# A conditional attention block whose two ends are reordered

## Chip, core and metric

One core of a Trainium2 chip. The time is that of the device in microseconds (us). Three runs of the kernel before gave 372.36, 374.06 and 375.03 us (median 374.06). The profile is one further execution.

## What is computed

For each of 16 batches x (256 tokens, 256 features), with one conditioning vector w per batch:

```
gamma, beta = w @ Wg.T + bg, w @ Wb.T + bb          # one row of 256 per batch
sln(h)  = gamma * ((h - mean) / sqrt(var + 1e-5) * ln_g + ln_b) + beta
q, k, v = sln(x) @ Wqkv.T + bqkv                    # 16 heads of 16 features
att     = softmax(q @ k.T) / 16 @ v
h1      = att @ Wp.T + bp + x
out     = sln(h1) + h1
```

All inputs and the output are float32. The kernel keeps that precision with matmuls in fp32r, by splitting each operand into a high part (the fp32r rounding) and a low part (what is left): three matmuls stand for one product. For the scores the four combinations of parts are stacked in the 128 rows of one contraction, and two more rows of it subtract the row maximum.

## The kernel before

Every engine has its own instruction list, written out by hand; semaphores join them. TensorE (PE) multiplies and transposes, ScalarE (ACT) takes exponentials and copies PSUM to SBUF, VectorE (DVE) takes maxima, norms and low parts, GpSimd (POOL) does small work on SBUF, SyncE (SP) issues most transfers. Each list runs in its order; an instruction that waits holds all behind it on its engine.

**Steps.** After a set-up, `steps(step, last=B + 2)` runs step b = -1 to 17 on every engine, each with 16 slots h, one per head. In step b PE computes the scores of batch b, head h, into `st0` or `st1` in turn (L838), and the same products for batch b+1 into `sa0` or `sa1` (`scores_max`, L825), of which DVE takes the row maxima (L573). ACT's exponential (L512) empties the score bank. `weigh` (L849) multiplies four heads' exponentials with V, three slots later, into `pv0` (heads 0 to 7) or `pv1`. The other work of neighbouring batches has fixed slots (L46 to L54): projections of Q and K of batch b+2 (L799) and of V of batch b+1 (L808), the transposes of the maxima (L889), `out_by_token` (L873), the transposes of `att`, the output projection of batch b-1 (L817), and gamma and beta of batch b-2 as rows of `gb` (L965). `between` (L713) is the same table for DVE: `residual` stages 0 to 5 are the sum h1, its statistics, mean and variance, epsilon, and the two halves of the second norm; `norm1` is the first norm; `low_qk`, `low_att` and `low_max` are low parts; `normalise` divides by the softmax sum.

**Stacks.** `qst` and `kst` hold the stacked parts of Q and K. `stack(a, g, t)` on SP (L267) sends the high parts of batch a, half g of the heads, t = 0 for Q and 1 for K, in two transfers of 128 KB, waits for the low parts and sends them in two more. For batch 0, K goes by ACT's queue (`stack_k0`, L530). POOL issues the two small transfers of the maxima rows (`maxima`, L315; `m_h` and `m_l`), which the scores of that half wait for (L842). The transfers of batch 1's first half go out in step -1, of its second half in step 0.

**Set-up.** PE keeps busy with matmuls on zeros (`warm_up`, 9 and 5 of them: `WARM`), waits for all of `vectors`, `cond`, `wg` and `wb` (`cond_in`, L1010), transposes the vectors, multiplies gamma and beta into one bank, transposes the normed x of batch 0 (`turn_x(0)`), then projects Q and K of batch 0 (`project_first`) once `hTl_ready` says that the low part of h is there. Then follow the transposes of gamma and beta to rows, `turn_x(1)`, the bias product `Wp.T @ bv + bp` (`rows_bias`, L905), and Q of batch 1. K of batch 1 comes in slots 0 to 3 of step -1. ACT rounds the weights and zeroes `qst` in four `clear_q` (L516), the last behind `high_q(1)`.

**End.** In step 15 there is no batch 16 to take maxima of: PE has scores, weighs, transposes and the projection of batch 14. Steps 16 and 17 hold the end of batch 15: last weigh, `evict_out`, transposes, `normalise`, transposes, `aT_h`, `low_att`, projection, `residual`. The rows `gb` of batches 14 and 15 are multiplied and copied there too, each ahead of the `h1b` sum on POOL (L377) that it is needed for.

Of the kernel before, what the change touches and what calls it, by code (L numbers as in the profile page):

```python
# [32 lines left out]
P = 128  # L33
# [15 lines left out]
WARM = (9, 5)  # L49
# [4 lines left out]
S_OT1, S_OT0 = 5, 13  # L54


def cond_block(nc, x, condT, vectors, WgT, WbT, WqkvT, WpT, bp, out):
    with ExitStack() as ctx:
# [27 lines left out]
        gb_part = sb("gb_part", [P, KT, B])  # L86
        gfull = sb("gfull", [P, KT, B])
# [32 lines left out]
        gb = sb("gb", [P, 2 * D])  # L120
        h1 = sb("h1", [P, TT, D])
# [11 lines left out]
        cond_in = sem("cond_in")  # L133
# [6 lines left out]
        max_in = [[sem(f"max_in{g}{p}") for p in range(2)] for g in range(2)]  # L140
        qpad_ready = sem("qpad_ready")
# [19 lines left out]
        gbpart_ready = sem("gbpart_ready")  # L161
        gfull_ready = sem("gfull_ready")
# [46 lines left out]
        h1_ready = sem("h1_ready")  # L209
        ln2_step = sem("ln2_step")  # L210
# [27 lines left out]

        def xbuf(a):

            return xa[:, a % NX]

        def steps(body, first=-1, last=B + 1):

            for b in range(first, last):
                body(b)
# [7 lines left out]
        def _(sp):  # L254
            wqkv_t = WqkvT.rearrange("(k p) n -> p k n", p=P)
            sp.dma_start(xbuf(0), x_t[0]).then_inc(x_in[0], 16)
            sp.dma_start(vrows[:], vectors).then_inc(cond_in, 16)
            sp.dma_start(cond[:], condT.rearrange("(k p) n -> p k n", p=P)).then_inc(cond_in, 16)
# [8 lines left out]
            def stack(a, g, t):  # L267

                if not has(a):
                    return  # L270
# [5 lines left out]
                s, p = stack_in[g][par(a)], par(a)  # L276
                dst, hi, lo = (qst, kst)[t], qk_h[:, p, t, g, :], qk_l[:, p, t, g, :]
                wait(sp, (qh_ready, kh_ready)[t], 1 * a + 1)
                for n in (0, 2) if t == 0 else (0, 1):
                    sp.dma_start(raw(dst[PART_ROW[n]:P:P // HD, p, g * HH:(g + 1) * HH, :]), raw(hi)).then_inc(s, 16)  # L280
                wait(sp, (ql_ready, kl_ready)[t], 1 * a + 1)
                for n in (1, 3) if t == 0 else (2, 3):
                    sp.dma_start(raw(dst[PART_ROW[n]:P:P // HD, p, g * HH:(g + 1) * HH, :]), raw(lo)).then_inc(s, 16)

            def step(b):
                if not first(b + 1):
                    stack(b + 1, 1, 0)
                    stack(b + 1, 1, 1)
# [4 lines left out]
                stack(b + 2, 0, 0)  # L293
                stack(b + 2, 0, 1)
# [11 lines left out]
            for p in range(2):  # L306
                sp.wait_ge(y_out[p], 16 * (B // 2))
# [760 lines left out]
```

## Time and profile before

| | us |
|---|---|
| median of three runs | 374.06 |
| the profiled execution's own time | 374.8 |
| its span, first to last instruction | 373.0 |
| PE busy | 351.7 (94%) |
| DVE busy | 305.7 (82%) |
| ACT busy | 248.7 (67%) |
| POOL busy | 162.8 (44%) |

Busy shares are means over stages that differ. The page's slices show that both ends are thinner than the middle (tenths of 40 equal slices, and PE's granted clock in tenths of full speed):

```profile
PE   8788999999999999999999999999999999999960
DVE  2779877789888888899898888888898978886563
ACT  6434677767776776777676767767776767677710
PEclk9969999999999999999999999999999999999975
```

"Granted clock" is 1.00 where PE may run at 2.4 GHz and 0.50 at 1.2 GHz. An idle time in brackets is that of the engine just before the group, with what ended it.

### The profile page before, as it was taken

Reading aid. Unit: us, or ns where it says so; the run is one execution under the profiler, and the core shown is the slowest. Engines: PE = TensorE matmul, PEld = TensorE weight load, DVE = VectorE, ACT = ScalarE, POOL = GpSimd, SP = SyncE. Lnnn points to the kernel's source line nnn. Section 1 sums busy time; section 2 is a strip of 40 time slices with the busy share of each in tenths; the row PEclk is TensorE's granted clock in tenths of the full one; section 3 lists DMA queues with packets and bytes.
Section 4 is the critical chain, followed back from the end, with each engine's and each line's share of the span. In section 5 each row is a group of like instructions: output and inputs, shape, how many; then the busy total and the mean of one; then the engine's idle time right before and its main releaser. Section 6 shows DMA issues by size and latency. Waiting matters only on the chain.

```text
span 373.0 us, 8969 instructions
## 1 busy us (share of the span) xinstructions
PE 351.7 (94%) x3161; PEld 291.4 (78%) x3161; DVE 305.7 (82%) x729; ACT 248.7 (67%) x487; POOL 162.8 (44%) x203
## 2 busy tenths in 40 slices
PE   8788999999999999999999999999999999999960
PEld 5566778888888888888888889888888888787640
DVE  2779877789888888899898888888898978886563
ACT  6434677767776776777676767767776767677710
POOL 6616443327262725435262627254352634062242
PEclk9969999999999999999999999999999999999975
DMA  7095445444354444555544544444554443410000
GB/s 265 28 219 153 108 117 144 117 137 123 111 142 123 127 121 126 143 145 143 143 105 126 143 123 127 115 134 140 144 142 118 108 136 102 133 45 30 31 28 28
DMA packets 45258, 44.69 MB, mean 120 GB/s; under 512 B 6015, under 2 KB 40846, under 8 KB 45214
## 3 DMA queue, kind: packets, MB, share of 16 engines
q1 hardware_dynamic: 41470, 42.02, 40.7%
q10 hardware_dynamic: 1696, 1.57, 1.7%
q0 software_dynamic: 2048, 0.53, 0.9%
q8 instruction: 25, 0.41, 0.5%
q14 instruction: 19, 0.16, 0.1%
HBM read 5.79 MB, written 4.19 MB: 27 GB/s over the span
## 4 chain that ended last, share of the span: by engine, by line
PE 88%; DVE 5%; issue 2%; ACT 2%; DMA 1%; POOL 0%; POOLq 0%; DVEq 0%; ACTq 0%
PE m L791 24%; PE pv L791 20%; PE st L791 19%; PE sa L791 17%; PE pv L880 4%; PE pv L988 2%; PE m L920 1%; DVE mx L573 1%; PE m L894 1%; DMA qst<-m_l 1%; ACT p L512 1%; DVE qk_l L608 1%; PE pv L894 0%; DVE y L689 0%; DVE xn L635 0%
## 5 line engine op out<-in xcount | busy, mean ns | idle before, releaser
L573 DVE TENSOR_REDUCE mx<-sa 128x2 f32<-128x512 f32 x256 | 171.9, 678 | 40.6 <-PE sa L791 39.8
L512 ACT ACTIVATE p<-st 128x512 f32<-128x512 f32 x256 | 150.8, 599 | 58.3 <-PE st L791 57.7
L791 PE MATMUL st<-qst,kst 128*128 128x256 f32 x512 | 111.9, 301 | 1.2 <-DMA qst<-m_l 0.6
L791 PE MATMUL sa<-kst,qst 126*128 126x256 f32 x512 | 104.8, 286 | 2.2 <-DVE mx L573 1.9
L791 PEld LDWEIGHTS st<-qst,kst 128*128 128x128 f32 x512 | 77.8, 189 | 29.0 <-ACT p L512 16.4
L791 PEld LDWEIGHTS sa<-kst,qst 126*128 126x128 f32 x512 | 79.4, 191 | 4.1 <-DVE mx L573 4.0
L323 POOL DMA_DIRECT2D qst<-m_h x32 | 18.1, 566 | 118.3 <-DVE m_l L582 118.3
L791 PE MATMUL pv<-p,v_st 128*32 128x256 f32 x1024 | 68.5, 385 | 0.3 <-ACT p L512 0.3
L791 PEld LDWEIGHTS pv<-p,v_st 128*32 128x32 f32 x1024 | 26.7, 109 | 20.0 <-ACT p L512 0.5
L791 PE MATMUL m<-hT_h,wqkv_h 128*128 128x256 f32 x128 | 38.6, 310 | 0.3 <-DVE hT_l L652 0.3
L791 PE MATMUL m<-hT_l,wqkv_h 128*128 128x256 f32 x128 | 35.8, 288 | 0.0
L791 PE MATMUL m<-hT_h,wqkv_l 128*128 128x256 f32 x128 | 35.6, 287 | 0.0
L332 POOL TENSOR_SCALAR xn<-xa,mv,rstd 128x256 f32<-128x256 f32 x28 | 34.0, 1216 | 0.4
L350 POOL TENSOR_TENSOR hT_l<-hT,hT_h 128x512 fp32r<-128x512 f32 x14 | 17.9, 1278 | 35.8 <-ACT hT_h L426 35.8
L364 POOL TENSOR_TENSOR rstd<-vare,minus_half 128x4 f32<-128x4 f32 (+1 forms) x19 | 17.3, 908 | 33.5 <-DVE vare L630 19.4
L462 ACT ACTIVATE oT<-pv 128x512 f32<-128x512 f32 x32 | 19.2, 599 | 15.9 <-PE pv L791 15.9
L608 DVE SCALAR_TENSOR_TENSOR qk_l<-m,vecs,qk_h 128x256 fp32r<-128x256 f32 x64 | 27.6, 473 | 2.1 <-ACT qk_h L442 2.1
L791 PEld LDWEIGHTS m<-hT_h,wqkv_h 128*128 128x128 f32 x128 | 24.9, 199 | 1.9 <-issue 1.9
L791 PEld LDWEIGHTS m<-hT_h,wqkv_l 128*128 128x128 f32 x128 | 24.5, 195 | 0.6
L791 PEld LDWEIGHTS m<-hT_l,wqkv_h 128*128 128x128 f32 x128 | 24.6, 197 | 0.0
L689 DVE SCALAR_TENSOR_TENSOR y<-h,mv,gb 128x256 f32<-128x256 f32 x32 | 24.4, 801 | 0.0
L791 PE MATMUL m<-wp_h,aT_h 128*128 128x256 f32 x64 | 20.0, 312 | 2.1 <-DVE aT_l L658 2.1
(104 smaller groups left out, 574.1 us busy)
## 6 DMA issues: line engine op xcount, KB each, us to landing
qst<-qk_h SPq DMA_DIRECT2D x64, 128.0 KB, 2.4
qst<-qk_l SPq DMA_DIRECT2D x64, 128.0 KB, 2.5
kst<-qk_h SPq DMA_DIRECT2D x60, 128.0 KB, 2.5
kst<-qk_l SPq DMA_DIRECT2D x60, 128.0 KB, 2.8
xa<-x_dram SPq DMA_DIRECT2D x16, 256.0 KB, 3.1
out_dram<-y SPq DMA_DIRECT2D x16, 256.0 KB, 2.1
wqkv<-WqkvT_dram SPq DMA_DIRECT2D x1, 512.0 KB, 5.3
kst<-qk_h ACTq DMA_DIRECT2D x4, 128.0 KB, 4.3
```

The source lines that it names most:

```text
L323: pool.dma_start(raw(qst[MAX_ROW + r:MAX_ROW + 1 + r, p, g * HH:(g + 1) * HH, :]) .rearrange("a h (t n) -> a (h t) n", t=TT), raw(m[:, g, ...
L332: o = pool.tensor_scalar(xn[:, t, :], xbuf(a)[:, t, :], mv[:, t, 0:1], rstd[:, 0, t:t + 1], ALU.subtract, ALU.mult)
L350: pool.tensor_tensor(hT_l[:, par(a)], hT[:], hT_h[:, par(a)], ALU.subtract).then_inc(hTl_ready, 1)
L364: pool.tensor_tensor(rstd[:, which], vare[:, which], minus_half[:, which], ALU.pow).then_inc(rstd_ready, 1)
L462: nc.scalar.activation(oT[:, g, :], pv_ps[g][:], ACT.Copy).then_inc(oT_ready, 1)
L512: nc.scalar.activation(p32[:, h % PR, :], st_ps[h % 2][:], ACT.Exp).then_inc(exp_done, 1)
L573: dve.tensor_reduce(mx[:, par(a), h // HH, (h % HH) * TT:(h % HH + 1) * TT], sa_ps[h % 2][:].rearrange("p (t n) -> p t n", t=TT), AX.X, AL ...
L608: o = dve.scalar_tensor_tensor(out=qk_l[:, par(a), t, g, :], in0=ps[:, g * N:(g + 1) * N], scalar=vecs[:, 4 + t, g:g + 1], in1=qk_h[:, par ...
L689: o = dve.scalar_tensor_tensor(out=y[:, par(a), t, :], in0=h1[:, t, :], scalar=mv2[:, t, 0:1], in1=gb[:, 0:D], op0=ALU.subtract, op1=ALU.mult)
L791: return nc.tensor.matmul(o, l, r, start=start, stop=stop)
L880: o = nc.tensor.transpose(pv_ps[g][:, t * N + c * P:t * N + (c + 1) * P], oT[:, g, c * N + t * P:c * N + (t + 1) * P], ident[:])
L988: o = nc.tensor.transpose(pv_ps[1][:, k * N + t * P:k * N + (t + 1) * P], att[:, t, k * P:(k + 1) * P], ident[:])
```

## The change

At the head:

- Loads: `cond` is issued ahead of `vectors`; three semaphores (`vrows_in`, `wg_in`, `wb_in`) take the place of `cond_in`. gamma and beta get a bank each. Their bias terms are worked out beforehand (`gb_add`), so bfull is one sum.
- PE's warm-ups are 8 and 4. `project_first` starts when the high part of h is there, and takes the low part after that. `rows_bias` moves ahead of `turn_x(1)`, and `bias_cols` on DVE far ahead. Q of batch 1: two quarters before step -1 and two in slots 0 and 1; K in slots 2 to 5; V of batch 0 in slots 9 and 10 (`V_FIRST`) instead of 7 to 9. The transpose of the first maxima goes to `pv1`.
- ACT: the fourth `clear_q` and the high part of the V weights move ahead of `high_q(0)`, the copy of the bias ahead of `high_q(1)`, `high_k(1)` from slot 4 to 6. ACT, not POOL, issues the first maxima rows.
- DVE: `low_qk` of K of batch 0 passes ahead of the norm of batch 1; both `low_qk` of batch 1 move from slots 1 and 5 to 8 and 9, behind the eight maxima of the first half.
- SP: `send` is one quarter of a stack; all high parts of batch 1 go out ahead of its low parts, and its second half in step -1. POOL fills `kst` of batch 1 in one piece ahead of `rstd_x(1)`.

At the end:

- Steps run to 15, and an ending is written out for each engine. In step 15 DVE makes the four copies from PSUM (oT twice, gb, aT_h) that ACT made, and the projection of batch 14 stands in slots 10 to 12 (`P_LAST`).
- The rows of gamma and beta for batches 14 and 15 are made in step 14 (`gb_t`, `S_GT`).
- Batch 15's second group of heads is handled by halves: its two weighs go to two banks; eviction, transposes, normalise, transposes and `aT_h` work on four heads or on one 128-row part; the projection adds the first part early (`project_half(0)`), then four warm-ups, then the second. h1, h1b, the last y and the output go by halves of the tokens.

```diff
-WARM = (9, 5)
+WARM = (8, 4)
+V_FIRST = (9, 9, 10, 10)
+WARM_END = 4
+P_LAST = (10, 11, 11, 12)
+S_GT = (4, 11)
...
-            stack(0, 0, 0)
-            stack(0, 1, 0)
-            steps(step, last=B + 2)
+            for g in range(2):
+                for low in range(2):
+                    send(0, g, 0, low)
+            for t in range(2):
+                for g in range(2):
+                    send(1, g, t, 0)
+            for t in range(2):
+                send(1, 0, t, 1)
+            steps(step)
+            wait(sp, y_ready, B - 1)
+            sp.dma_start(out_t[B - 2], y[:, par(B - 2)]).then_inc(y_out[par(B - 2)], 16)
+            for t in range(TT):
+                sp.wait_ge(yt_ready, t + 1)
+                sp.dma_start(out_t[B - 1][:, t, :], y[:, par(B - 1), t, :]).then_inc(y_out[par(B - 1)], 16)
...
+                    if h == S_MT0 + 1 and first(b + 1):
+                        for r, m, ready in ((0, m_h, mh_ready), (1, m_l, ml_ready)):
+                            act.wait_ge(ready, 1)
+                            act.dma_start(raw(qst[MAX_ROW + r:MAX_ROW + 1 + r, 0, 0:HH, :])
+                                          .rearrange("a h (t n) -> a (h t) n", t=TT),
+                                          raw(m[:, 0, :])).then_inc(max_first, 16)
...
             high_h_direct(0)
             clear_q(1, 0)
+            clear_q(1, 1)
+            act.wait_ge(wv_in, 16)
+            nc.scalar.activation(wqkv_h[:, :, 2 * D:3 * D], wqkv[:, :, 2 * D:3 * D], ACT.Copy).then_inc(wvh_ready, 1)
             act.wait_ge(vecs_ready, 1)
             high_q(0)
...
-                    between[(1, 0)] = [lambda: low_qk(1, 0, m0, qh_ready, ql_ready)]
-                    between[(5, 0)] = [lambda: low_qk(1, 1, m1, kh_ready, kl_ready)]
-                    between[(9, 0)] = [lambda: low_max(0, 0)]
+                    between[(8, 0)] = [lambda: low_qk(1, 0, m0, qh_ready, ql_ready), lambda: low_max(0, 0)]
+                    between[(9, 0)] = [lambda: low_qk(1, 1, m1, kh_ready, kl_ready)]
+                if last(b):
+                    between[(3, 1)] = [lambda: evict_out_last(b - 1, 1)]
+                    between[(4, 1)] = [lambda: evict_rows_last(b - 2)]
+                    between[(9, 1)] = [lambda: high_att_last(b - 1), lambda: low_att(b - 1)]
+                    between[(11, 0)] = [lambda: evict_out_last(b, 0)]
+                    between[(12, 1)] = [lambda: residual(b - 1, 0)]
+                    between[(15, 0)] = [lambda: residual(b - 1, 1)]
+                    between[(15, 1)] = [lambda: residual(b - 1, 2), lambda: residual(b - 1, 3)]
...
+            low_att_half(0)
+            residual(B - 2, 4)
+            normalise_half(0)
+            normalise_half(1)
+            residual(B - 2, 5)
+            low_att_half(1)
+            wait(dve, xdb_ready, B)
+            wait(dve, h1b_ready, B - 1)
+            for t in range(TT):
+                wait(dve, projt_done, t + 1)
+                dve.tensor_tensor(h1[:, t, :], st_ps[t][:, 0:D], xbuf(B - 1)[:, t, :], ALU.add).then_inc(h1t_ready, 1)
...
+            weigh(B - 1, 2)
+            pe.wait_ge(att_ready, 2 * B - 1)
+            for t in range(TT):
+                o = nc.tensor.transpose(sa_ps[1][:, t * P:(t + 1) * P], att[:, t, 0:P], ident[:])
+            o.then_inc(aT0_done, 1)
+            weigh(B - 1, 3)
...
+            project_half(0)
+            pe.wait_ge(attt_ready, 2)
+            for t in range(TT):
+                o = nc.tensor.transpose(pv_ps[1][:, t * P:(t + 1) * P], att[:, t, P:2 * P], ident[:])
+            o.then_inc(aT1_done, 1)
+            pe.wait_ge(h1_ready, B - 1)
+            for _ in range(WARM_END):
+                mm(m1[:], zeros[:, 0:P], zeros[:], True, True)
+            project_half(1)
```

## Rows read from the trace of the kernel before

**Rows 1.** Stretches (us); busy time and count of each engine, granted clock, DMA.
```profile
39.10:319.00 279.90, 279.70 (x2657) 238.38 (x2658) 244.18 (x582) 203.22 (x411) 126.63 (x148) 1.00 0.47 128
...
340.00:354.20 14.20, 13.47 (x124) 9.10 (x122) 7.29 (x19) 11.08 (x22) 4.80 (x6) 1.00 0.06 21
```
**Rows 2.** In order of time, set-up: start, length, engine, line, operation.
```profile
1.46 4.02 PE L791 MATMUL sa<-zeros 128*128 128x512 bf16 x9 [1.46 <-DVE zeros L746]
...
5.41 0.18 PEld L1012 LDWEIGHTS pv<-ident,vrows 14*128 14x128 f32 x1 [0.84 <-DMA cond<-condT_dram]
...
9.06 1.09 PE L920 MATMUL st<-ident,xn 128*128 128x128 f32 x4
...
10.07 0.36 DVE L763 SCALAR_TENSOR_TENSOR bfull<-pv,vecs,gb_part 128x16 f32<-128x16 f32 x2
...
12.62 1.20 PE L791 MATMUL m<-hT_h,wqkv_h 128*128 128x256 f32 x4 [0.34 <-DVE hT_l L652]
...
16.00 0.84 ACT L442 ACTIVATE qk_h<-m,vecs 128x256 fp32r<-128x256 f32 x2 [2.59 <-PE m L791]
```
**Rows 3.** Stretches again, where PE idles or runs at the lower clock.
```profile
16.80:19.30 2.50, 0.02 (x1) 0.00 (x0) 2.42 (x5) 0.77 (x3) 1.99 (x4) 1.00 0.32 78
...
20.50:22.30 1.80, 1.73 (x5) 0.99 (x5) 0.71 (x2) 0.93 (x2) 0.00 (x0) 0.61 1.13 223
...
25.50:27.50 2.00, 2.00 (x11) 1.94 (x10) 1.10 (x3) 1.10 (x3) 0.57 (x1) 0.50 1.10 223
...
360.30:362.00 1.70, 1.69 (x8) 1.69 (x9) 0.75 (x2) 0.00 (x0) 0.00 (x0) 0.50 0.05 17
```
**Rows 4.** In order of time, 17 to 29 us.
```profile
17.67 1.58 DVE L635 TENSOR_SCALAR xn<-xa,mv,rstd 128x256 f32<-128x256 f32 x2
...
20.07 1.20 ACTq L535 DMA_DIRECT2D kst<-qk_l  x2
...
27.12 1.91 ACT L516 ACTIVATE qst<-ones 128x2048 fp32r<-128x2048 f32 x1
```
**Rows 5.** Instructions on tile `kst`, 16 to 28 us: its transfers.
```profile
DMA to landing us min/median/max: 3.2/4.7/5.5
```
**Rows 6.** In order of time, step -1 and the first scores.
```profile
26.96 0.69 DVE L573 TENSOR_REDUCE mx<-sa 128x2 f32<-128x512 f32 x1 [0.87 <-PE sa L791]
...
30.86 0.88 DVE L608 SCALAR_TENSOR_TENSOR qk_l<-m,vecs,qk_h 128x256 fp32r<-128x256 f32 x2
...
31.65 1.97 DVE L573 TENSOR_REDUCE mx<-sa 128x2 f32<-128x512 f32 x3
...
33.87 0.69 DVE L573 TENSOR_REDUCE mx<-sa 128x2 f32<-128x512 f32 x1 [0.25 <-PE sa L791]
...
34.70 4.55 DVE L573 TENSOR_REDUCE mx<-sa 128x2 f32<-128x512 f32 x7
...
38.20 1.27 POOL L350 TENSOR_TENSOR hT_l<-hT,hT_h 128x512 fp32r<-128x512 f32 x1 [1.90 <-ACT hT_h L426]
...
39.10 0.50 PE L791 MATMUL st<-qst,kst 128*128 128x256 f32 x2 [0.58 <-DMA qst<-m_l]
```
**Rows 7.** In order of time, step 15 and the end.
```profile
342.88 0.39 PE L791 MATMUL pv<-gb_hl,pick_b 128*128 128x512 f32 x1
...
353.63 0.60 ACT L512 ACTIVATE p<-st 128x512 f32<-128x512 f32 x1 [0.84 <-PE st L791]
...
354.28 1.07 PE L791 MATMUL pv<-p,v_st 128*32 128x256 f32 x16 [0.34 <-ACT p L512]
...
357.39 2.26 DVE L689 SCALAR_TENSOR_TENSOR y<-h,mv,gb 128x256 f32<-128x256 f32 x2
...
364.01 0.75 DVE L674 BATCH_NORM_STATS2 stats<-h 128x6 f32<-128x256 f32 x2
...
367.57 0.88 DVE L697 SCALAR_TENSOR_TENSOR y<-y,rstd,h1b 128x256 f32<-128x256 f32 x2 [1.53 <-POOL h1b L377]
```
**Rows 8.** The page's part 6, DMA issues: KB each, median us to landing.
```profile
out_dram<-y SPq DMA_DIRECT2D x16, 256.0 KB, 2.1
```

More of the change, by code:

```diff
@@ L237, in par, with max_sent, last, steps @@
             return a % 2
+        def max_sent(a, g):
+            return 32 * (half(a) + (1 if g or par(a) else 0)) if a >= 0 else 0
+        def last(a):
+            return a == B - 1
         def xbuf(a):
             return xa[:, a % NX]
-        def steps(body, first=-1, last=B + 1):
+        def steps(body, first=-1, last=B):
             for b in range(first, last):
@@ L275, in stack @@
                     sp.wait_ge(kpad_ready, a + 1)
[L276 to L283, printed above, removed]
+                wait(sp, ((qh_ready, ql_ready), (kh_ready, kl_ready))[t][low], 1 * a + 1)
+                src = (qk_h, qk_l)[low][:, p, t, g, :]
+                for n in (low, low + 2) if t == 0 else (2 * low, 2 * low + 1):
+                    sp.dma_start(raw((qst, kst)[t][PART_ROW[n]:P:P // HD, p, g * HH:(g + 1) * HH, :]),
+                                 raw(src)).then_inc(s, 16)
+            def stack(a, g):
+                if not has(a):
+                    return
+                for t in range(2):
+                    for low in range(2):
+                        send(a, g, t, low)
             def step(b):
-                if not first(b + 1):
-                    stack(b + 1, 1, 0)
-                    stack(b + 1, 1, 1)
+                if has(b - 1) or has(b) and not first(b):
+                    stack(b + 1, 1)
                 if has(b + 4) and has(b):
@@ L465, in step @@
                 for h in range(H):
-                    if h == S_O1:
+                    if h == S_O1 and not last(b):
                         evict_out(b - 1, 1)
-                    if h == S_O0:
+                    if h == S_O0 and not last(b):
                         evict_out(b, 0)
-                    if h == S_GB + 1 and has(b - 2):
+                    if h - 1 in S_GT and last(b + 1):
+                        i = S_GT.index(h - 1)
+                        wait(act, gbt_done, i + 1)
+                        nc.scalar.activation(gb_t[:, i, :], m0[:], ACT.Copy).then_inc(gbt_ready, 1)
+                    if h == S_GB + 1 and has(b - 2) and not last(b):
                         wait(act, gb_done, 1 * (b - 2) + 1)
@@ L841, in scores @@
                 if h % HH == 0:
-                    wait(pe, max_in[h // HH][p], 32 * (half(b) + 1))
+                    if first(b) and h == 0:
+                        pe.wait_ge(max_first, 32)
+                    else:
+                        wait(pe, max_in[h // HH][p], max_sent(b, h // HH))
                 wait(pe, exp_done, 16 * b + h - 1)
@@ L851, in weigh @@
                 p, g, c = par(b), q // 2, q % 2 * N
+                bank = pv_ps[g]
+                if last(b) and q == 3:
+                    bank, c = m0, 0
                 wait(pe, exp_done, 16 * b + 4 * q + 4)
@@ L858, in weigh @@
                     wait(pe, att_ready, 2 * b + g - 1)
+                if last(b) and q == 3:
+                    pe.wait_ge(gbt_ready, 2)
                 if q == 0:
@@ L947, in step @@
                     a, j = (b, h - LAG) if h >= LAG else (b - 1, h - LAG + H)
-                    if has(a) and j % 4 == 3:
+                    if has(a) and j % 4 == 3 and not (last(a) and j // 4 == 2):
                         weigh(a, j // 4)
```

251 lines of the change are left out of this document (190 added, 61 removed).

## The prediction

> **What bounds the kernel now.** I read busy time by stretches first, then the instructions in order of time at both ends. From 39.1 to 319 us TensorE (PE) is busy 279.7 of 279.9 us at full granted clock, and in the last full batch (step 15, 340.0 to 354.2) 13.5 of 14.2 us [rows 1]. The change leaves the steps between alone, so I forecast nothing there. What can move is the 39.1 us ahead of the first score matmul, step 15, and what follows it: the last weigh starts at 354.28, the last y ends at 367.57 + 0.88 = 368.45 [rows 7], the span at 373.0.
>
> **Head, first part.** PE's transpose of `vrows` sat 0.84 us behind the `cond` transfer [rows 2]. Now it waits for `vrows` alone, and one 0.43 us warm-up is gone (nine took 4.02 us): PE is 0.4 us ahead. gamma and beta keep their eight matmuls each, so `turn_x(0)` ends at 9.75 instead of 9.06 + 1.09 = 10.15 [rows 2]. The bfull chain (old end 10.43) loses its common wait: gamma work runs beside the beta matmuls, and the four small operations added on DVE (2 on gb_add, 2 for bias_cols, some 0.8 us) run before gamma arrives at 7.2. So `hT` starts at 9.85 rather than 10.48. The first projection now asks for hT_h (about 11.05: two ACT halves after 9.85), where hT_l released it at 12.62 [rows 2]; four warm-ups of 0.43 from 9.6 end near 11.3. Up to Q's eviction at 16.00 PE needed 3.4 us [rows 2]; started 1.3 us earlier, with more of them at the low clock, I let its matmuls end 1.2 us earlier, Q at 14.8 and all 24 at 15.2.
>
> **ACT gives half of that back.** Ahead of `high_q(0)` it now has a second `clear_q` of 1.91 us (old place 27.12 [rows 4]) and the V weights' high part (128 x 512, 0.6 like an exp of that size [rows 7]). 11.05 + 1.9 + 1.9 + 0.6 = 15.45 against 16.00 [rows 2]: 0.55 us ahead. Then `low_qk` of K passes ahead of the 1.58 us of xn [rows 4]: ACT's queue, which stands on kl_ready, issues kst<-qk_l at 18.7 instead of 20.07 [rows 4], and gets to hT_h(1) 1.3 us sooner. Hence hT_l(1) is ready at 21.95 instead of 23.3. PE starts Q of batch 1 at 22.05. Of its twelve matmuls (0.21 each at granted 0.50: eight in 1.69 us [rows 3]) only six stand ahead of the first maxima. SP issues the same transfers in another order: batch 0 first, then all high parts of batch 1. Nothing that batch 0 needs is behind a later wait. The last K part for heads 0 to 7 is issued by 19.95; landings took 3.2 to 5.5, median 4.7 [rows 5], so 23.1 to 25.4. I take 23.5, since the two engines issue the same bytes 0.5 us sooner: PE begins the maxima at 23.5, DVE at 24.0 where it began at 26.96 [rows 6].
>
> **Bias in PE's gap.** PE sat idle 2.5 us from 16.8; at 20.5 to 22.3 the clock had fallen to 0.61 on average, at 25.5 to 27.5 it was 0.50, that is 1.2 GHz [rows 3]. The six bias matmuls now fill about 15.9 to 17.3, which hides them; without that gap they would cost those 1.4 us. Idle remains: 17.3 to 19.0 for xn, 19.6 to 22.05 for hT_l, 4.1 us in two pieces against one of 2.5 and a short one: I take it that the clock still falls. The Trainium skill, "TensorE: Matmul & The Clock Gate", section "What's actually happening", says that activity releases the throttle and that the moment of the change is not tied to the kernel's start and varies from run to run; by it the gap's outcome can differ between runs of one program. That is the first rival.
>
> **First step (maxima of batch 0).** At 1.2 GHz a head with 2 sa and 3 projection matmuls costs PE 1.07 us, DVE's maximum takes 0.655 (1.97/3 [rows 6]). Three or four heads go at PE's pace, the rest at DVE's: the eighth maximum ends near 30.5. Before it was 31.65 + 1.97 = 33.6 with two `low_qk` (0.87, 0.88 [rows 6]) in front; a shift of -3.1. Those two now stand behind it: +1.75 back, and the 0.25 us that DVE waited ahead of the ninth [rows 6], with V matmuls in PE's slot 7, goes away. V moves to slots 9 and 10, under DVE's extra 0.88. The maxima rows go out by ACT's queue directly; m_l was written ahead of the seven maxima that start at 34.70, and its transfer released the first scores at 39.10 after 0.58 us of idle [rows 6]; now m_l is there at 31.2 against a need at 37.4, so that transfer leaves the path even at 5.5 us. Next late are DVE's last seven maxima (4.55 us) and hT_l(2) on POOL, 38.20 + 1.27 = 39.47 [rows 6], which moves with the ninth maximum. Both shift by -3.1 + 1.75 - 0.25 = -1.6. K's low part of batch 1 is ready at 33.1, issued by 34.5 and needed at 37.5; a landing of 3.2 from 33.9 fits, one of 5.5 would cost 2. **Head: -1.6 us**, bounds +0.1 and -2.8.
>
> **Step 14.** Two more 512-column matmuls for gb_t with their loads: the like one took 0.39 from start to end [rows 7]; overlapped with its neighbours I charge a little over half, 0.22, and PE is the bound: +0.45, from 0 to 1. ACT's two copies lie in its third of idle time; SP and POOL get one small copy each way.
>
> **Step 15.** ACT had 16 exps of 0.60 [rows 7], and between them copies of the same 128 x 512 for oT, gb, aT_h and oT. Four copies to DVE (about 0.69 each, what a maximum over the same bank takes [rows 6]) take 2.4 us from ACT. But score banks are two, and PE's weighs (1.07) already hold the exps up; following the two-bank rule head by head, the last exp starts at 352.85 instead of 353.63 [rows 7]. The projection of batch 14 moves up into slots 10 to 12 and eats what the copies give. weigh(15,2) moves behind the loop but before weigh(15,3), so that one ends at about 355.0 instead of 354.28 + 1.07 = 355.35: only 0.4 gained here.
>
> **Tail, by halves.** Before, from 355.4: oT, transposes, rec, att, transposes, aT_h, then DVE was held by y of batch 14 (2.26 us, started 357.39, twice its free 0.88 [rows 7]), aT_l, 12 matmuls at granted 0.50 (from 360.31 on, [rows 3]), h1, statistics, y, POOL's rstd and h1b (DVE idle 1.53 on it), last y. After, in the same clock: second half of oT 355.0 to 355.4, its transposes to 355.8. DVE: low_att_half(0) 354.4 to 354.8, y of 14 from 354.8. POOL adds h1b(14) at 354.6 to 355.8, so I charge the slowed pair, 1.9, not 0.88: to 356.7. Two normalise halves, an estimate of 0.55 each: 357.8. Transposes, aT_h half: 358.6. Second y of 14 (0.87) runs meanwhile; low_att_half(1) to 359.05. The first half of the projection and four warm-ups cover PE's wait, so PE idles under 1.5 us at a time and I keep the clock at full: six matmuls 0.7 (half of 6 x 0.21, and a little), with h1 (2 x 0.4) started after three: 360.35. Statistics, aggregate, vare: 1.2 us, as from 364.01 on [rows 7], 361.6; y 0.88 to 362.5. POOL's h1b halves run during the statistics, rstd (0.88) beside y. Last y 362.5 to 363.4. Old 368.45: -5.05, of which 0.4 is step 15, 1.4 the earlier projection, 1.9 its half length and full clock, 1.4 h1b off the path. Output follows: 256 KB took 2.1 from issue [rows 8]; two of 128 KB, the second no earlier than the last y: 0 to -1, I take -0.3. **Step 15 and tail: -5.35**, bounds -3.7 and -6.3 (y of 14 free of POOL: another -0.95).
>
> **Sum.** -1.6 + 0.45 - 5.35 = -6.5 us. The profiled run took 374.8 (span 373.0 and 1.8 around it), 0.74 above the median of three; 374.8 - 6.5 = 368.3 on its terms, 367.6 on the median's.
>
> **Rivals.**
> Clock stays up in the head (0.17): the bias fill leaves shorter gaps; for it speaks the 1.00 that still stood at the end of 2.5 us of idle, against it the 0.50 after [rows 3]. Then DVE paces all 16 maxima from 23.5, eighth at 29.3: -2.8 in the head, 366.4.
> Tail only (0.13): batch 1's low parts land late, or K's landing eats the start; the head's -1.6 is nil: 369.2.
> Clock drops in the tail (0.13): the four warm-ups become 1.7 us, outlasting DVE's 359.05 by 0.8, and six matmuls cost 0.6 more: -5.35 becomes -3.95, 369.0; with DVE's in-order queue also late by a us, 370.2.
> No effect (0.06): the ends are as long as before because something I take for hidden is not, 373 to 375.
> Slower (0.04), one mechanism: with 12 warm-ups instead of 14 before 11.3 us and less dense work, PE's clock does not rise and steps 0 on run at 0.50. In a PE-bound step each us spent at half clock loses half a us; against a gain of 6.5, 13 us of it turn the sign. The row of 25.5 to 27.5 shows that busy PE can stand at 0.50 [rows 3]; full clock over all of 39.1 to 319 speaks against. At 21 us of it, a step: 378.
> The rest (0.47) is the sum as it stands.
>
> **Numbers.** 1% is 3.7 us, about what can be told from no change. Faster by more, under 370.3: the sum 0.47, clock up 0.17, tail only 0.12, most of the clock drop 0.07: 0.83. Within 1%: 0.12; slower: 0.05. Range 364.4 to 371.2: the gain bound of both ends (-2.8 - 6.3) sits just outside at the low side, the double miss in the tail inside at the high side.
>
> **What would show it.** PE's first projection near 11.3 and ending near 15.2; qk_h at 15.4; first maximum at 24, the eighth ended at 30.5, scores at 37.5 with hT_l(2), not a transfer, as PE's releaser; granted clock between 20 and 27. The last exp should start 12.8 us after step 15's first scores, and the last y end 10.5 us behind it (14.8 before). In the tail: y of 14 at 1.9, PE's clock at the second half projection, POOL no longer named ahead of the last y. A head shift of zero, or step 15 no shorter, would make the forecast wrong.

## The result and the profile after

The changed kernel took 368.32 us (median of four runs, 368.09 to 369.82) against 374.54 for the kernel before: the ratio is 0.985, with an interval of 0.980 to 0.990. That is 1.5% faster, 6.2 us. The forecast was 367.6, 364.4 to 371.2. The profiled execution took 368.27, with a span of 366.4: 6.6 us under the profiled one before.

The page's first part after (busy us, share, instructions). Of the 6.6 us of span, 4.6 are PE's busy time (351.7 before; nearly the same number of instructions, fewer of them at the lower clock) and 2.0 its idle time; DVE is busy for 4.5 us more than before.

```profile
PE 347.1 (95%) x3162; PEld 288.1 (79%) x3163; DVE 310.2 (85%) x738; ACT 247.0 (67%) x485; POOL 161.9 (44%) x202
```

The head after, in order of time, with the instructions that answer to [rows 2] and [rows 6]:

```profile
5.81 0.23 PE L1201 MATMUL pv<-ident,vrows 14*128 14x14 f32 x1 [0.85 <-DMA vrows<-vectors_dram]
5.97 1.06 PE L960 MATMUL pv<-cond,wg 128*128 128x16 f32 x8
...
8.33 1.91 PE L960 MATMUL sa<-zeros 128*128 128x512 bf16 x4
...
10.06 1.85 PE L960 MATMUL m<-hT_h,wqkv_h 128*128 128x256 f32 x8
...
13.98 0.83 ACT L517 ACTIVATE qk_h<-m,vecs 128x256 fp32r<-128x256 f32 x2
...
22.03 0.64 PE L960 MATMUL sa<-kst,qst 126*128 126x256 f32 x2
...
24.84 4.10 DVE L668 TENSOR_REDUCE mx<-sa 128x2 f32<-128x512 f32 x6 [0.38 <-PE sa L960]
...
35.02 1.28 POOL L401 TENSOR_TENSOR hT_l<-hT,hT_h 128x512 fp32r<-128x512 f32 x1 [4.68 <-ACT hT_h L498]
35.18 0.40 PE L960 MATMUL st<-qst,kst 128*128 128x256 f32 x2
...
36.35 0.39 PE L960 MATMUL m<-hT_h,wqkv_h 128*128 128x256 f32 x1 [0.26 <-POOL hT_l L401]
```

The eighth maximum ends at 28.94 (before 33.6), the first scores wait for no transfer, and the first projection of step 0 starts at 36.35 with `hT_l` as its releaser, which is the releaser that was forecast; before, it started at 39.69.

How the lead then runs on is best read at one instruction that comes twice in each step: PE's transpose of the maxima. Of its 32 times I give the lead over the kernel before (worked out as the difference of the two traces): 3.23 us in step 0, 3.27 at 125.5 us, 3.04 from 136.4 us on, 2.96 when step 14 begins, 2.58 at its end (340.7 before, 338.12 after). So 0.23 is lost in one piece in step 4 and 0.38 in step 14. The start of the last weigh is 1.81 ahead (354.28 before, 352.47 after): another 0.77 is lost in step 15. It has two parts. From the first scores of step 15 to the last exp it is 351.21 - 337.44 = 13.77 us, where it was 353.63 - 340.02 = 13.61: 0.16 lost. From the last exp to the start of the last weigh it is 1.26 instead of 0.65, another 0.61, since the weigh of the third group and two transposes now stand between them. The last y is 6.37 ahead, the span 6.6. The end therefore gained 4.56 behind the start of the last weigh, and step 15, which was to gain, lost.

Step 15 and the end after, by engines, in order of time; the part of it that answers to [rows 7]:

```profile
341.77 1.29 POOL L432 TENSOR_TENSOR h1b<-h,gb 128x512 f32<-128x512 f32 x1
...
342.76 3.44 DVE L789 SCALAR_TENSOR_TENSOR y<-h,mv,gb 128x256 f32<-128x256 f32 x2
343.01 1.27 POOL L392 TENSOR_TENSOR xa<-xa,bias_b 128x512 f32<-128x512 f32 x1
...
344.25 1.27 POOL L472 TENSOR_TENSOR xa<-xa,bias_b 128x512 f32<-128x512 f32 x1
...
346.13 0.68 DVE L818 CAST aT_h<-pv 128x512 fp32r<-128x512 f32 x1
...
347.58 0.39 PE L960 MATMUL m<-wp_h,aT_h 128*128 128x256 f32 x1 [1.14 <-DVE aT_l L753]
...
348.48 0.60 ACT L597 ACTIVATE p<-st 128x512 f32<-128x512 f32 x1 [2.40 <-PE st L960]
...
352.47 1.07 PE L960 MATMUL m<-p,v_st 128*32 128x256 f32 x16
...
353.34 1.69 DVE L789 SCALAR_TENSOR_TENSOR y<-h,mv,gb_t 128x256 f32<-128x256 f32 x2
...
355.96 0.44 PE L1248 MATMUL pv<-ident,att 128*128 128x128 f32 x2 [0.76 <-DVE att L928]
...
357.33 0.38 PE L960 MATMUL st<-wp_h,aT_h 128*128 128x256 f32 x1
...
361.20 0.88 DVE L954 SCALAR_TENSOR_TENSOR y<-y,rstd,h1b 128x256 f32<-128x256 f32 x2 [0.30 <-POOL rstd L488]
```

The reader should follow one line of cause: POOL makes three whole additions one behind the other from 341.77 to 345.52; DVE's pair of y, 0.88 when alone, takes 3.44; DVE's copy of aT_h, next in its queue, comes at 346.13, so PE stands 1.14 us for aT_l, and with it the next scores: ACT idles 2.40 us ahead of an exp. The run "POOL late" below tests this.

### The profile page after: what moved, and what is told of

Same layout as the page of the kernel before. It is cut to its first block, busy times and chain, and to the rows that moved or that the text cites. A ratio compares the mean times of both kernels' runs of the same rounds, so it can differ in the third digit from the quotient of the medians.

```text
span 366.4 us, 9039 instructions
## 1 busy us (share of the span) xinstructions
PE 347.1 (95%) x3162; PEld 288.1 (79%) x3163; DVE 310.2 (85%) x738; ACT 247.0 (67%) x485; POOL 161.9 (44%) x202
## 3 DMA queue, kind: packets, MB, share of 16 engines
q10 hardware_dynamic: 1760, 1.59, 1.6%
## 4 chain that ended last, share of the span: by engine, by line
PE 85%; DVE 5%; ACT 3%; DMA 2%; issue 1%; ACTq 1%; POOL 1%; SPq 0%; POOLq 0%; DVEq 0%
PE m L960 24%; PE st L960 19%; PE pv L960 18%; PE sa L960 16%; PE pv L1057 4%; PE pv L1169 2%; PE m L1097 2%; DMA wqkv<-WqkvT_dram 2%; DVE mx L668 1%; DVE y L789 1%; PE m L1071 1%; ACT qst L601 1%; ACTq L620 1%; ACT p L597 1%; ACT hT_h L611 0%
## 5 line engine op out<-in xcount | busy, mean ns | idle before, releaser
L960 PE MATMUL pv<-p,v_st 128*32 128x256 f32 x1008 | 67.5, 385 | 0.0
L537 ACT ACTIVATE oT<-pv 128x512 f32<-128x512 f32 x29 | 17.4, 599 | 14.0 <-PE pv L960 14.0
L415 POOL TENSOR_TENSOR rstd<-vare,minus_half 128x4 f32<-128x4 f32 (+1 forms) x17 | 15.7, 923 | 19.2 <-DVE vare L725 19.1
L789 DVE SCALAR_TENSOR_TENSOR y<-h,mv,gb 128x256 f32<-128x256 f32 x28 | 23.2, 866 | 0.0
L960 PE MATMUL m<-wqkv_h,hT_h 128*128 128x256 f32 x64 | 19.3, 301 | 0.2 <-DVE qk_l L703 0.2
```

The lines of the kernel that those rows point to most:

```text
L415: pool.tensor_tensor(rstd[:, which], vare[:, which], minus_half[:, which], ALU.pow).then_inc(rstd_ready, 1)
L537: nc.scalar.activation(oT[:, g, :], pv_ps[g][:], ACT.Copy).then_inc(oT_ready, 1)
L789: o = dve.scalar_tensor_tensor(out=y[:, par(a), t, :], in0=h1[:, t, :], scalar=mv2[:, t, 0:1], in1=gam[:, 0:D], op0=ALU.subtract, op1=ALU. ...
L960: return nc.tensor.matmul(o, l, r, start=start, stop=stop)
```

## The experiments

Each run's time is a median, of four runs (ten for head only, five for best); "before" is the kernel before, measured together with it. Runs of one edited kernel differ by up to 2.4 us (368.00 to 370.36 for "loads together"), so medians a few tenths apart tell nothing. Where tenths count I use two distances inside each trace, since the time also holds the head's luck (below). The first is from the first maxima matmul to the first projection of step 0 ("step -1"); the second from the transpose of batch 15's second maxima, a little into step 15, to the start of the last y ("end"). In the changed kernel they are 36.35 - 22.03 = 14.32 and 361.20 - 338.12 = 23.08 us. The six traces with the changed kernel's very ending have 23.08 to 23.10, so the second repeats to a few hundredths; the first varies from 14.06 to 14.62 in the twelve with its order of step -1.

| run | time | before | step -1 | end | first maxima |
|---|---|---|---|---|---|
| before | 374.54 | | 13.53 | 26.87 | 26.16 |
| changed | 368.32 | 374.54 | 14.32 | 23.08 | 22.03 |
| head only | 372.92 | 374.06 | 14.39 | 26.9 | 22.93 |
| POOL late | 368.51 | 374.06 | 14.33 | 21.9 | 23.64 |
| ACT copies | 368.41 | 374.06 | 14.06 | 22.3 | 23.88 |
| no end warm-ups | 370.03 | 374.06 | 14.46 | 23.1 | 23.69 |
| both | 367.53 | 374.57 | 14.14 | 22.3 | 22.08 |
| halves first | 366.28 | 374.57 | 14.62 | 21.0 | 22.17 |
| low parts early | 370.95 | 374.57 | 15.71 | 23.1 | 23.80 |
| wait for hT_l | 369.59 | 374.57 | 14.23 | 23.1 | 23.01 |
| bias late | 369.83 | 373.18 | 14.39 | 23.1 | 23.79 |
| vectors first | 368.44 | 373.18 | 14.54 | 23.1 | 22.27 |
| loads together | 369.27 | 373.18 | 14.54 | 23.1 | 23.66 |
| best | 365.91 | 373.18 | 14.42 | 21.0 | 21.99 |

**Head alone.**

```diff
-            return a == B - 1          # last(a)
+            return False
-        def steps(body, first=-1, last=B):
+        def steps(body, first=-1, last=B + 2):
```
and the written-out endings of all engines, `gb_t` and its `pick_t` are taken out.

> The head of the change with the end of the kernel before (steps to 17, ACT's evictions, whole batch 15, POOL as before). If the two ends simply add, step 0 starts as early as in the changed kernel (first scores near 35.2, 3.3 us ahead at the first projection of step 0), the end costs what it did, and the time is 3.2 us under the kernel before: 371.3. If what the head gained beyond my 1.6 us is the luck of the clock in one run, the lead at step 0 is 1.6 to 2 us here: 372.7. If the head's lead is given back in the steps between, the second-half maxima transposes of later batches lose it again: 374.

Measured: 372.92, ratio 0.9958 (0.9936 to 0.9981) over ten runs, so 1.1 to 1.6 us, near my second theory's time (372.7), though the trace leads by 2.27 us in step 0, more than the 1.6 to 2 of that theory. It keeps the lead to the end, 2.39 at the last transpose: nothing is given back when the changed end is absent. In the traces the two ends add. The changed kernel's span is 370.43 - 366.44 = 3.99 us shorter: 0.96 is a faster head in that execution, 3.80 the end (26.88 against 23.08), and 0.77 goes off for steps 4 and 14. So the end with what it costs is worth 3.0 us. The difference of the medians, 372.92 - 368.32 = 4.6, is larger, since the two sets of runs also differ in the head's luck.

The head's time does not hang on PE alone. Here the weights for the first projection landed late, and ACT, which rounds them ahead of `hT_h`, started a microsecond after the changed kernel's 8.00:

```profile
9.03 1.06 ACT L602 ACTIVATE wqkv_h<-wqkv 128x1024 fp32r<-128x1024 f32 x1 [2.28 <-DMA wqkv<-WqkvT_dram]
```

The first projection therefore began at 11.10 instead of 10.06; the maxima began at 22.93.

**POOL late.**

```diff
                 if first(a):
                     pool.wait_ge(bias_ready, 1)
+                if a == B - 2:
+                    wait(pool, ln2_step, 4 * (B - 2))
...
             wait(pool, xn_ready, B)
+            wait(pool, y_ready, B - 2)
```

> As the changed kernel, but POOL's sum of bias and x for batch 14 waits until DVE's first y of batch 13 is made, and the one for batch 15 until the second. Theory (POOL holds DVE's second port for whole additions): y of batch 13, 3.44 us for the pair in the changed kernel, falls to 2.2 or less, DVE's copy of aT_h comes over 1 us earlier, PE's 1.14 us wait for aT_l in slot 10 goes, step 15 is about 1.1 us shorter and the time 367.2. Rival (the DVE copies themselves, in one in-order queue, make aT_l late): y gets shorter, but aT_l still comes after the weigh of slot 10, 368.3, no change. Second rival: the late additions collide with DVE's low_att and second y instead, and take it all back.

DVE and POOL in order of time, in slots 8 and 9 of step 15:

```profile
344.20 0.98 DVE L792 SCALAR_TENSOR_TENSOR y<-h,mv,gb 128x256 f32<-128x256 f32 x2
345.26 1.27 POOL L394 TENSOR_TENSOR xa<-xa,bias_b 128x512 f32<-128x512 f32 x1 [0.77 <-DVE y L792]
...
345.92 0.69 DVE L821 CAST aT_h<-pv 128x512 fp32r<-128x512 f32 x1 [0.73 <-PE pv L1172]
```

The pair of y takes 0.98 instead of 3.44, DVE's copy now waits 0.73 us for PE and not PE for DVE, and the end is 1.21 us shorter (361.43 - 339.56 = 21.87; the expectations below say 21.83). From the first scores of step 15 to the last exp it now takes 351.44 - 338.88 = 12.56 us, against 13.77 in the changed kernel and 13.61 before the change. The theory holds by the trace. The time, 368.51, does not show it: this profiled run had the slow head (first maxima at 23.64), 1.6 us behind the changed kernel's.

**ACT copies again in step 15.**

```diff
-                    if h == S_O1 and not last(b):
+                    if h == S_O1:
...
-                    between[(3, 1)] = [lambda: evict_out_last(b - 1, 1)]
-                    between[(4, 1)] = [lambda: evict_rows_last(b - 2)]
-                    between[(11, 0)] = [lambda: evict_out_last(b, 0)]
```
and likewise `gb` and `aT_h`.

> As the changed kernel, but in step 15 ACT makes the four copies again (oT twice, gb, aT_h), as before the change; DVE does not. Theory that the move to DVE gave nothing because y of batch 13 then blocked it: step 15 takes the same 13.8 us from first scores to last exp within 0.5, time 368.0 to 368.8. Rival (the move did help and the block only ate into it): without it the copies stand between exps, step 15 is 0.8 to 1.5 us longer, 369.5. Third: DVE's copies were the cause of the loss, then this is 0.8 us faster, 367.5.

Time 368.41; the end is 22.28, 0.8 shorter than in the changed kernel, and step 15 takes 12.96 us from first scores to last exp, not 13.8: my theory falls, and the third theory has the size. But DVE's copies cost nothing by themselves, as the next run shows: the pair of y here takes 1.92, as in the kernel before, and POOL's additions 1.47 and 1.46 instead of 1.27.

```profile
343.25 1.28 POOL L432 TENSOR_TENSOR h1b<-h,gb 128x512 f32<-128x512 f32 x1
344.49 1.47 POOL L392 TENSOR_TENSOR xa<-xa,bias_b 128x512 f32<-128x512 f32 x1
345.92 1.46 POOL L472 TENSOR_TENSOR xa<-xa,bias_b 128x512 f32<-128x512 f32 x1
```

These are POOL's three additions in order of time. The two engines alternate here; in the changed kernel POOL's three follow each other and shut DVE out. Why the order differs is not shown.

**Both edits.**

> As the changed kernel with both edits: POOL's two additions late, and ACT making the four copies of step 15. Measured from the transpose of batch 15's second maxima to the start of the last y: 23.08 us in the changed kernel, 21.83 with POOL late, 22.28 with ACT copying. Theory (the DVE copies help by about 0.45 once y of batch 13 isn't blocked): 22.2 to 22.4 here. Rival (the copies are worth nothing, only the block counted): 21.8. Third (both were separate losses): 21.0 to 21.4.

Time 367.53; end 360.28 - 338.03 = 22.25, the theory's number. With POOL out of the way, DVE's copies are worth 22.25 - 21.87 = 0.4 us, a gain that the changed kernel does not get. It is not the 0.4 of the prediction: that was all of step 15, an exp 0.78 earlier less what the order of the last weighs costs.

**No warm-ups at the end.**

```diff
-WARM_END = 4
+WARM_END = 0
```

> As the changed kernel without the four warm-up matmuls ahead of the second half of the last projection. If they keep the clock up, PE's gap of about 2.3 us drops it, the six matmuls take 1.3 instead of 0.7 us, and the time is 368.9 to 369. If the clock outlasts this gap, nothing changes, 368.3, and the warm-ups are idle ornament; if the warm-ups themselves were in the way of the projection, it is 0.1 to 0.3 us faster.

PE's first matmul of the second half, in order of time, and then the stretches around it (granted clock behind the five engines):

```profile
359.07 0.36 PE L960 MATMUL st<-wp_h,aT_h 128*128 128x256 f32 x1 [1.02 <-DVE aT_l L920]
```

```profile
358.00:359.50 1.50, 0.48 (x4) 0.46 (x4) 0.77 (x2) 0.38 (x1) 0.00 (x0) 1.00 0.19 72
359.50:361.00 1.50, 0.51 (x5) 0.31 (x3) 1.20 (x4) 0.00 (x0) 0.61 (x1) 1.00 0.28 102
```

The granted clock is 1.00 through the second half of the projection in both, and the end is the same 23.1. In this run the warm-ups did nothing. The time, 370.03 against 368.32, is not explained by its end; the profiled run had the slow head (23.69), which is 1.7 us of it. Whether the clock falls in some of the other runs is open.

**Halves first.** On top of POOL late, DVE's ending is reordered:

```diff
             low_att_half(0)
-            residual(B - 2, 4)
             normalise_half(0)
             normalise_half(1)
-            residual(B - 2, 5)
+            residual(B - 2, 4)
             low_att_half(1)
+            residual(B - 2, 5)
```

> POOL's additions late, and in the ending DVE's normalise halves ahead of the first y of batch 14, the second y behind low_att_half(1). Theory: y of batch 14 (1.69 us, under POOL's h1b) stood 353.34 to 355.03 ahead of the normalise halves on the path; with it behind them att is ready 0.8 us earlier, PE's idle time ahead of its transposes goes from 0.76 to nearly nothing, and the stretch from the last maxima transpose to the last y is 21.0 to 21.2 instead of 21.83; time 367.6. Rival: y only moves its 0.9 to 1.7 us ahead of low_att_half(1), which then becomes late, no change, 368.4.

Time 366.28, ratio 0.9785 (0.9729 to 0.9840); end 359.50 - 338.47 = 21.03, 0.84 less than with POOL late alone. In DVE's list, in order of time, it now stands 0.53 us ahead of the halves for PE, and y of batch 14, no longer under POOL's h1b, takes 0.87 where it took 1.69 (with POOL late too):

```profile
353.09 0.21 DVE L929 RECIPROCAL rec<-sa 128x8 f32<-128x8 f32 x1 [0.53 <-PE sa L1235]
...
354.11 0.87 DVE L792 SCALAR_TENSOR_TENSOR y<-h,mv,gb_t 128x256 f32<-128x256 f32 x2
355.14 0.42 DVE L923 TENSOR_TENSOR aT_l<-pv,aT_h 128x256 fp32r<-128x256 f32 x1 [0.16 <-ACT aT_h L660]
```

**Low parts early.**

```diff
-                    between[(8, 0)] = [lambda: low_qk(1, 0, m0, qh_ready, ql_ready), lambda: low_max(0, 0)]
-                    between[(9, 0)] = [lambda: low_qk(1, 1, m1, kh_ready, kl_ready)]
+                    between[(3, 0)] = [lambda: low_qk(1, 0, m0, qh_ready, ql_ready)]
+                    between[(7, 0)] = [lambda: low_qk(1, 1, m1, kh_ready, kl_ready)]
+                    between[(8, 0)] = [lambda: low_max(0, 0)]
```

> As the changed kernel, but DVE makes batch 1's low parts of Q and K among the first half's maxima again (ahead of maxima 3 and 7), not behind all eight. From the first maxima matmul to the first projection of step 0 the changed kernel took 14.3 us (14.32, 14.39, 14.33, 14.06, 14.46 in five runs with this head). Theory (DVE's work in step -1 is the same in any order and bounds it): 14.3 within 0.3, no change in time. Rival (the order was worth the 1 to 1.5 us that the maxima rows' transfer was late before): scores wait for the transfer again, 15.3 or more and time 369.5.

My theory falls: step -1 takes 15.71, not 14.3, and the time is 370.95. The rival's size is right, its cause is not: the first scores at 38.33 waited for no transfer. DVE now idles in the places to which the change had moved the low parts (DVE in order of time, its idle time in brackets):

```profile
32.88 0.28 DVE L677 SCALAR_TENSOR_TENSOR m_l<-pv,m_h 16x128 fp32r<-16x128 f32 x1 [0.78 <-ACT m_h L507]
...
35.30 0.69 DVE L668 TENSOR_REDUCE mx<-sa 128x2 f32<-128x512 f32 x1 [0.25 <-PE sa L961]
...
36.65 2.58 DVE L668 TENSOR_REDUCE mx<-sa 128x2 f32<-128x512 f32 x4 [0.66 <-PE sa L961]
```

0.78 + 0.25 + 0.66 = 1.7 us of idle against 0.23 in the same part of the changed kernel: behind the eighth maximum DVE must wait for PE's transpose and ACT's rounding anyway, and two slots later for the V matmuls. The low parts fill these two holes. That is what the move is worth: 1.3 to 1.4 us.

**The first projection waits for hT_l again.**

```diff
-            pe.wait_ge(hTh_ready, 1)
+            pe.wait_ge(hTl_ready, 1)
             pe.wait_ge(gfull_ready, 1)
             project_first()
```

> As the changed kernel, but the first projection waits for the low part of h. hT_l ended 0.8 us after PE started. Theory: PE starts 0.7 later, 24 matmuls end 0.7 later but ACT stands until 13.98 to 15.4 on clear_q and the V weights, so Q's eviction moves only 0 to 0.4 and the first maxima with it: 368.3 to 368.7, nothing to be told apart. Rival: PE, not ACT, is the releaser of qk_h and all 0.7 us stay in the time: 369.0 with qk_h idle on PE.

Time 369.59. qk_h here starts at 15.02 and stood 0.79 us for PE; in the changed kernel it starts the moment ACT is free (13.98). For this trace the rival is right. But PE's matmuls fell to the low clock halfway in this run (the last 16 of them in 3.6 us), so how much of the 1.0 us is the wait and how much the clock stays open. The time and the first maxima (23.01) do not settle it: head only, without this edit, has 22.93.

**Bias behind turn_x(1).**

```diff
-            rows_bias()
             turn_x(1)
+            rows_bias()
```

> As the changed kernel, but rows_bias behind turn_x(1) again (bias_cols stays early). Prediction's step: the early gap hides 1.4 us. Theory now: PE idles 2.5 us for hT_l(1) behind turn_x(1) in the changed kernel (18.1 to 20.6), so the bias fits there too, at 1.3 us in a full clock and 2.9 in the low one. The first maxima then move by 0 to 0.5 us: 368.3 to 368.8. Rival: PE idle before it loses the clock sooner, the bias takes 2.9 us, and the time is 369.5 or more.

PE in order of time, from the transposes to the projection of batch 1:

```profile
19.11 0.66 PE L1097 MATMUL st<-ident,xn 128*128 128x128 f32 x4 [2.68 <-DVE xn L730]
19.61 1.03 PE L960 MATMUL pv<-wp,bias_cols 128*128 128x256 f32 x4
20.57 0.69 PE L960 MATMUL pv<-row,ones 1*128 1x256 f32 x2
22.52 0.36 PE L960 MATMUL m<-hT_h,wqkv_h 128*128 128x256 f32 x1 [1.26 <-DVE hT_l L747]
```

The bias fits into the later gap too, at full clock, with 1.26 us left. First maxima at 23.79 against 23.64 to 23.88 in the other runs with this kind of head: the place of the bias is worth nothing that shows. 369.83 is the time of such a head. But something did change: with the bias in the later gap PE's granted clock stayed at 1.00 until 24.28, where in the five other heads of this kind it had fallen at 19.5 to 21.0. The six matmuls of Q of batch 1 ran at full clock, and then PE waited for a transfer:

```profile
23.79 0.48 PE L960 MATMUL sa<-kst,qst 126*128 126x256 f32 x2 [0.33 <-DMA kst<-qk_l]
```

The clock also stood at 1.00 through this gap in head only and in the run that waits for hT_l, and both waited 0.34 us at the same place. So a clock that stays up here gains next to nothing, because the low part of K lands only then.

**Loads.** Two edits: `vectors` issued ahead of `cond` (as before the change); and PE waiting for all four transfers at once.

```diff
-            sp.dma_start(cond[:], ...).then_inc(wg_in, 16)
             sp.dma_start(vrows[:], vectors).then_inc(vrows_in, 16)
+            sp.dma_start(cond[:], ...).then_inc(wg_in, 16)
```

> As the changed kernel, but vectors are issued ahead of cond, as before the change. PE's transpose of vrows started at 5.25 to 5.85 in the runs with cond first, 5.41 in the kernel before, where all four transfers were waited for. Theory: first in line, vrows lands near 5.0 and the transpose starts there; gamma then waits for cond, which lands last at 5.4 to 5.8; turn_x(0) starts no earlier: no change, 368.3. Rival: the transpose's latency was on the path, all is 0.3 to 0.5 us earlier, too little to tell apart in the time but plain in the trace.

```diff
             pe.wait_ge(vrows_in, 16)
+            pe.wait_ge(wg_in, 32)
+            pe.wait_ge(wb_in, 16)
```

> As the changed kernel, but PE waits for vectors, cond, wg and wb together ahead of its first transpose, which takes back what separate semaphores give. Theory: the four land within 0.3 us of each other, so that the transpose starts at 5.4 to 5.9 as in the changed kernel, no change, 368.3. Rival: wb, the last issued on ACT's queue, lands later than vrows and the start goes to 6.3 or more: 369.

With vectors first, the transpose starts at 4.99 instead of 5.81 (the range over runs with cond first is 5.25 to 5.89), and then PE waits 1.59 us for ACT's hT_h ahead of the projection at 10.28: nothing gained, 368.44. (ACT started to round the weights only at 8.22, when they had landed.) With one common wait it starts at 5.64, inside that range, and the time is 369.27 (368.00 to 370.36): no difference that can be told. In these traces separate semaphores gain nothing.

**Best.** Halves first, POOL late, vectors first, and POOL's two pick copies moved:

```diff
-                    if h in S_GT and b == 4:
...
+            pool.wait_ge(pick_ready, 1)
+            for i in range(2):
+                pool.tensor_copy(pick_t[:, i, :], pick[:, B - 2 + i:B - 1 + i]
+                                 .broadcast_to([P, P])).then_inc(pickt_ready, 1)
             pool.wait_ge(wph_ready, 1)
```

> The changed kernel with POOL's additions late, the normalise halves first, vectors issued ahead of cond, and the two copies of the pick columns on POOL made in its idle time in the set-up rather than in step 4. The first two together gave 366.28. Theory: the pick copies lost 0.23 us in step 4 (lead 3.27 at 128.8, 3.04 at 139.5 us); without them the lead over the kernel before, measured at the maxima transposes, stays the same to within 0.05 us from step 1 to step 13, and the time is 366.0 or a little less. Rival: the loss in step 4 has another cause and stays: 366.3.

365.91 (365.81 to 366.13), ratio 0.980 (0.978 to 0.983): 7.3 us under the kernel before and 2.4 under the changed one. The lead is 3.18 in step 0, 3.22 before and 3.23 after the place in step 4, and 3.33 when step 14 begins: the small copies on POOL had cost PE 0.23 us. Head only, which has no such copies, agrees: 2.31 before and 2.32 after. The first copy is enough, and it works by the pair of engines of step 15. These are POOL and DVE, first in the changed kernel, then here:

```profile
122.15 0.28 POOL L422 CAST pick_t<-pick 128x128 fp32r<-128x128 f32 x1
...
126.09 1.28 POOL L392 TENSOR_TENSOR xa<-xa,bias_b 128x512 f32<-128x512 f32 x1
126.20 1.84 DVE L789 SCALAR_TENSOR_TENSOR y<-h,mv,gb 128x256 f32<-128x256 f32 x2
```

```profile
125.90 1.27 POOL L394 TENSOR_TENSOR xa<-xa,bias_b 128x512 f32<-128x512 f32 x1
126.25 1.61 DVE L792 SCALAR_TENSOR_TENSOR y<-h,mv,gb 128x256 f32<-128x256 f32 x2
```

The copy puts POOL's next additions 0.2 us later, so more of one lies under DVE's pair of y, which takes 1.84 instead of 1.61.

## Why the prediction was right, step by step

**Right, by the steps that were given.** The sum said -6.5; the time moved by -6.2, the spans by -6.6. The scores no longer wait for the maxima's transfer; `hT_l` on POOL is what PE waits for; the ending from last weigh to last y took 13.1 us [rows 7] and now 361.20 + 0.88 - 353.54 = 8.54, where 8.4 was forecast; PE's clock stayed at 1.00 in it; y of batch 14 stood under POOL's addition (1.69, forecast 1.9). One sign there failed: POOL is still named ahead of the last y, with 0.30. Step 14 cost 0.38 (0.45); head only, without its two matmuls, lost nothing there. Output: -0.2 (-0.3).

The signs that the prediction named, in the changed kernel's trace and in that of POOL late, which has the same head in its slower kind:

| | forecast | changed | POOL late |
|---|---|---|---|
| first projection, start and end | 11.3, 15.2 | 10.06, 13.81 | 11.69, 15.46 |
| qk_h | 15.4 | 13.98 | 15.61 |
| first maximum on DVE | 24 | 22.82 | 24.44 |
| eighth ended | 30.5 | 28.94 | 30.56 |
| first scores | 37.5 | 35.18 | 36.79 |
| step 15's first scores to last exp | 12.8 | 13.77 | 12.56 |
| last exp to end of last y | 10.5 | 10.87 | 10.87 |

**Head: right for one of two kinds of execution.** In six of the thirteen traces of the changed kernel and its variants (POOL late, ACT copies, no end warm-ups, low parts early, bias late, loads together) the gamma matmuls ran slow (eight in 1.89 us) and the maxima began at 23.6 to 23.9: my 23.5. Five of these, all but low parts early, have their first projection of step 0 between 37.94 and 38.20, a lead of 1.5 to 1.75 against my 1.6. The trace of the kernel before is of this kind too, so this compares like with like. In the other seven, the changed kernel's profile among them, PE had reached full clock by gamma, gamma and beta took 0.8 us less each, and the maxima began at 22.0 to 23.0, a lead of 2.4 to 3.5. That the profiled execution of the changed kernel leads by 3.3 is luck, and it lies outside the bound of -2.8 that the prediction gave the head. This was not one of my rivals: I had placed the luck of the clock in the gap at 17 to 22 us, where the granted clock fell in the changed kernel as I had said (0.63 at 18 to 19.5, 0.50 from 19.5 to 24). The rival that it stays up there (366.4) came true in three traces and gained next to nothing, since PE then waited for the low part of K (bias late, above). The vectors' step had the wrong sign: I gave -0.4 for the transpose, which came 0.4 later (5.81 against 5.41 [rows 2]), since `cond` had been put in front. It cost nothing. And I priced the low parts behind the maxima as pure cost (+1.75) balanced by what stood in front; their worth, filling DVE's holes, came only with the experiment.

**Wrong: step 15.** The prediction said that "step 15 no shorter, would make the forecast wrong", and it is no shorter: the last exp was to come 0.78 us sooner within the step and came 0.16 later. The order of the last weighs, which the forecast's times put at 0.4, cost 0.61. So 0.4 forecast as gained became 0.77 lost. The step that failed is the list of POOL's work: the first addition of the new ending, bias plus x of batch 15, has nothing to wait for and runs right behind that of batch 14. I charged POOL's contention for y of batch 14, and left it out for y of batch 13, some 10 us earlier, though [rows 7] priced it and 345.43 with 1.92 us stood in the same trace. With both additions held back (POOL late) the same stretch takes 12.56 us, a little better than the 12.8 forecast: apart from POOL the step was sized well. The Trainium skill, "SBUF — State Buffer", section "SBUF: two separate sides", says of the port pair that DVE and GpSimd share that it is an exclusive lock held for a whole instruction, and that the loser fully blocks. The trace agrees that DVE is held for whole additions: the first of the pair ran 3.05 us, from 342.76 to 345.81, 0.3 behind the end of the third addition (1.29, 1.27 and 1.27 us). That DVE is not served between two of them is what this trace adds; in the run with ACT's copies it was.

**Missed, small.** The pick copies: "SP and POOL get one small copy each way" at no cost; measured 0.23, by the way shown under "Best". And the low end of the range: the two ends' bounds, -2.8 - 6.3, make 365.0 from 374.06, which is inside the range of 364.4 to 371.2 and not just outside it.

The errors nearly cancel in the profiled execution: the head gave 1.65 us more than forecast, and steps 4 and 15 took 1.4 more. That the sum is so close is luck in this sense. Over the runs, in which the head is sometimes the slower one, the time came out 0.7 above the forecast.

## What to carry to other kernels

When an engine's list is cut loose from its slots, look for the first instruction in the new tail that has no wait: it will run at once, and on POOL it can hold VectorE up where nobody looks. An instruction moved "behind" others is not only late: ask which waits it falls into, since an engine that must wait there anyway does it for nothing. And measure the parts of a kernel by distances within the trace: here the first maxima begin anywhere from 22.03 to 23.88 us in traces with the same head, mostly by when TensorE's clock rises, and one execution's trace does not tell which kind the others were.

## What the runs showed of the hardware

- Nearly the same head ran in two ways. PE was at 1.2 GHz in the warm-ups from 1.46 us (0.43 for 512 columns) in all traces. In seven it rose at 4.4 to 5.7 us and did gamma and beta at full rate (eight matmuls in 1.04 to 1.09 us), and in four of these fell back before or in the projection; in six, and in the kernel before, it did them slow (1.89) and rose at 12.7 to 14.2. The first maxima follow it: 22.0 to 23.0 against 23.6 to 23.9. The Trainium skill, "TensorE: Matmul & The Clock Gate", "What's actually happening", lets the moment vary from run to run; these traces agree that it varies.
- The granted clock is listed as 1.00 for 1.4 to 5.4 us, where the warm-ups ran at half rate, and in the kernel before also for 5.6 to 9.0, where gamma and beta did. At the start of a run the length of the matmuls tells the clock, not that column.
- At the end of the kernel without warm-ups, PE idled 1.02 us and stayed at 1.00. With 2.13 us of idle at the end of the kernel before, it was at 0.50 after [rows 3].
- VectorE and GpSimd, when each slows the other, can alternate or not: POOL's additions 1.47 and 1.46 with y at 1.92 in one kernel, 1.27, 1.27 and 1.29 with y at 3.44 in another.
